# Attention and routed experts on one core: value products a slot later in the last two groups, routing of the last batch but one moved later, last tables in eight steps

## What is computed

```
x = x + (softmax(q @ k.T / sqrt(16)) @ v) @ wo.T + bo      # q from layernorm(x); k, v from ctx
z = layernorm(x)
probs = softmax((z @ Wg + bg) / 5);  vals, idx = top_k(probs, 2)
gates = vals / (sum(vals) + 1e-9), on the two experts chosen
x = x + sum_e gates[e] * (gelu(z @ W1[e] + b1[e]) @ W2[e] + b2[e])
```

## Time and profile before

| | us |
|---|---|
| three runs | 808.95, 812.42, 813.84 |
| profiled execution | 810.08, of which its span 808.4 |
| busy in the span | PE 750.2, PE weight loads 447.4, DVE 612.7, ACT 455.7, POOL 395.0 |
| attention, to the end of the last value product | about 0 to 534 |
| experts | about 535 to 808 |
| mean granted clock of PE | 0.976 of full speed |

### The profile page before, as it was taken

One profiled execution on the slowest core, in us unless ns is written; L12 is line 12 of the kernel. 1 busy time (PEld: TensorE's weight loads), 2 busy tenths in 40 slices (PEclk: granted clock), 3 DMA queues, 4 the chain that ended last, 5 costly groups with the idle time before them and its releaser, 6 DMA issues.

```text
span 808.4 us, 16197 instructions
## 1 busy us (share of the span) xinstructions
PE 750.2 (93%) x4634; PEld 447.4 (55%) x4634; DVE 612.7 (76%) x1126; ACT 455.7 (56%) x663; POOL 395.0 (49%) x357
## 2 busy tenths in 40 slices
PE   7599999999999999999999988779999989999995
PEld 3233434444443444444444433348999879998994
DVE  6786778798797788788788787556786887767774
ACT  2056766776776766776766664663345334444441
POOL 6506143647637728728725613343344455344444
PEclk9679999999999999999999999899999999999998
DMA  6766756757766757757667567775454456444441
GB/s 205 219 172 200 205 154 226 216 173 241 223 185 239 210 179 258 193 177 252 193 180 252 164 164 249 279 269 119 74 96 73 82 130 112 74 73 75 77 70 12
DMA packets 90659, 136.23 MB, mean 169 GB/s; under 512 B 15456, under 2 KB 49216, under 8 KB 90192
## 3 DMA queue, kind: packets, MB, share of 16 engines
q1 hardware_dynamic: 76592, 117.33, 48.3%
q0 software_dynamic: 13296, 17.09, 12.0%
q10 hardware_dynamic: 688, 0.79, 0.3%
HBM read 71.25 MB, written 64.04 MB: 167 GB/s over the span
## 4 chain that ended last, share of the span: by engine, by line
PE 69%; DMA 8%; DVE 8%; issue 6%; ACT 5%; POOL 2%; POOLq 1%; SPq 0%; DVEq 0%; another core or an unknown queue 0%; ACTq 0%
PE ps_pv L1536 13%; PE ring L1523 10%; PE ring L1667 9%; PE ring L1685 9%; PE ring L1510 6%; PE ps_x L1567 6%; DMA out<-y_sb,xs 6%; DVE negm L1086 4%; PE ps_x L1585 4%; PE ps_x L1577 3%; ACT probs L1014 3%; PE ring L1676 3%; PE ps_x L1595 2%; PE ps_x L1554 1%; PE ps_pv L1658 1%
## 5 line engine op out<-in xcount | busy, mean ns | idle before, releaser
L1086 DVE TENSOR_REDUCE negm<-ring 128x2 f32<-128x1024 f32 x256 | 310.4, 1223 | 76.4 <-PE ring L1510 70.7
L1014 ACT ACTIVATE probs<-ring 128x1024 f32<-128x1024 f32 x256 | 260.4, 1024 | 95.5 <-PE ring L1523 81.5
L902 POOL DMA_INDIRECT out<-y_sb,xs x71 | 110.2, 1552 | 137.8 <-DMA out<-y_sb,xs 75.2
L1536 PE MATMUL ps_pv<-probs,v_aug 128*32 128x512 f32 x1024 | 139.8, 619 | 5.5 <-ACT probs L1014 5.5
L1523 PE MATMUL ring<-kq 64*128 64x512 f32 x512 | 127.7, 498 | 8.5 <-DVE negm L1086 8.3
L1510 PE MATMUL ring<-kq 64*128 64x512 f32 x512 | 110.6, 432 | 15.2 <-ACT probs L1014 5.4
L1523 PEld LDWEIGHTS ring<-kq 64*128 64x128 f32 x512 | 48.3, 187 | 110.7 <-issue 75.6
L1047 ACT CAST xsT_hi<-ps_pv 128x256 fp32r<-128x256 f32 x70 | 26.1, 373 | 129.8 <-PE ps_pv L1658 126.0
L793 POOL DMA_INDIRECT xs_dram<-xg,rows x64 | 64.0, 1001 | 58.6 <-DVEq L1254 33.8
L1685 PE MATMUL ring<-w_hi,hT_hi 128*128 x284 | 85.3, 300 | 0.1
L1685 PE MATMUL ring<-w_lo,hT_hi 128*128 x284 | 80.1, 282 | 0.0
(11 more groups left out here) (193 smaller groups left out, 1202.4 us busy)
## 6 DMA issues: line engine op xcount, KB each, us to landing
kq<-k_dram SPq DMA_DIRECT2D x64, 192.0 KB
kq<-q_dram SPq DMA_DIRECT2D x64, 192.0 KB
xs<-xs_dram SPq DMA_DIRECT2D x71, 132.5 KB
k_dram<-qk_hi SPq DMA_DIRECT2D x32, 256.0 KB
q_dram<-qk_hi SPq DMA_DIRECT2D x32, 256.0 KB, 2.8
o_dram<-oT SPq DMA_DIRECT2D x32, 256.0 KB
w_dram<-w_sb SPq DMA_DIRECT2D x12, 512.0 KB
w_hi<-w_dram SPq DMA_DIRECT2D x12, 512.0 KB
```

Source lines behind the costliest of these rows:

```text
L902: pool.indirect_dma_start(out=out, out_offset=bass.IndirectOffsetOnAxis(ap=xs[j % AHEAD][:, TOKEN:TOKEN + 1].bitcast(I32), axis=0), in_=y_ ...
L1014: nc.scalar.activation(probs[kt][:, 2 * jp:2 * jp + 2, :], ring[PLACE["ST", u, p] % RINGS][:], ACT.Exp).then_inc(exp_done, 1)
L1086: nc.vector.tensor_reduce(negm[:, v % 2, :, jp, kt], ring[PLACE["MX", v, p] % RINGS][:], AX.X, ALU.max, negate=True).then_inc(max_free, 1)
L1536: mm = nc.tensor.matmul(ps_pv[2 * DH * j:2 * DH * (j + 1), :], v_aug[:, kt, HPG * g + j, :], probs[kt][:, j, :], start=(kt == 0), stop=(kt ...
```

## The change

1. In groups 30 and 31 the value product of key tile kt is issued at slot 2 kt + 3 (after that slot's `score_t`), and the last one at slot 1 of the next group. ACT's copy of the group's sum (`take_o`) moves with it. For group 31 the last one stays after `turn_x(0)`.
2. Batch 6: `XG0`, `XG1`, `LG` go from (2, 5), (2, 6), (2, 7) to (2, 7), (3, 0), (3, 1). The route steps go from (3, 1) to (3, 4) to (3, 4) to (3, 7), ACT's exponential of the logits from (3, 0) to (3, 3). `PX` goes from (3, 5) to turn 0 of the expert loop. `turn_x(0)` waits for `LG` in place of `PX`.
3. Batch 5 in group (0, p) of batch 7: `second` from (0, 3) to (0, 4), `gates` from (0, 4) to (0, 6).
4. `last_tables` is cut into eight parts of two to six instructions, in turns 27 to 34. Its instructions are the same.

```diff
 LAST_POST = {(1, 3): "OP0", (1, 4): "OP1", (1, 5): "OP2", (1, 6): "OP3",
-             (2, 5): "XG0", (2, 6): "XG1", (2, 7): "LG", (3, 5): "PX"}
+             (2, 7): "XG0", (3, 0): "XG1", (3, 1): "LG"}
-LAST_ROUTE = {(0, 1): "softmax", (0, 2): "first", (0, 3): "second", (0, 4): "gates"}
-LAST_ROUTE_POST = {(3, 1): "softmax", (3, 2): "first", (3, 3): "second", (3, 4): "gates"}
+LAST_ROUTE = {(0, 1): "softmax", (0, 2): "first", (0, 4): "second", (0, 6): "gates"}
+LAST_ROUTE_POST = {(3, 4): "softmax", (3, 5): "first", (3, 6): "second", (3, 7): "gates"}
-TAIL_PE = {6: "OP0", ...
+TAIL_PE = {0: "PX", 6: "OP0", ...
-TAIL_TABLES = {27: "tiles", 28: "past", 29: "rows"}
+TAIL_TABLES = {27 + n: n for n in range(8)}
+def tail_batch(j):
+    return B - 2 if j == 0 else 1 if TAIL_PE[j] == "CN" else B - 1
+def late(u):
+    return u >= G - 2
 # ACT
-                        if p == 0 and u > 0:
+                        if u > 0 and p == (1 if late(u - 1) else 0):
                             take_o(u - 1)
-                        if (g, p) == (3, 0) and i == B - 1:
+                        if (g, p) == (3, 3) and i == B - 1:
                             route_exp(i - 1)
 # PE
-                        if p == 0 and u > 0:
+                        if u > 0 and p == (1 if late(u - 1) else 0):
                             pv(u - 1, NT - 1)
-                        if p in (2, 4, 6):
-                            pv(u, p // 2 - 1)
+                        if p in ((3, 5, 7) if late(u) else (2, 4, 6)):
+                            pv(u, (p - 2) // 2)
                 if j == 0:
-                    pe.wait_ge(done["PX"], B - 1)
+                    pe.wait_ge(done["LG"], B - 1)
```

More of the change, by code:

```diff
@@ L92 @@
 TILES2 = TILES - TILES1
-TAIL_PE = {6: "OP0", 7: "OP1", 8: "OP2", 9: "OP3", 17: "XG0", 18: "XG1", 19: "LG", 25: "PX", 26: "CN"}
+TAIL_PE = {0: "PX", 6: "OP0", 7: "OP1", 8: "OP2", 9: "OP3", 17: "XG0", 18: "XG1", 19: "LG", 25: "PX", 26: "CN"}
 TAIL_LN2 = {10: "stats0", 11: "stats1", 12: "sums"}
 TAIL_ROUTE = {21: "softmax", 22: "first", 23: "second", 24: "gates"}
-TAIL_TABLES = {27: "tiles", 28: "past", 29: "rows"}
+TAIL_TABLES = {27 + n: n for n in range(8)}
 TAIL_RECIP, TAIL_NORMALISE, TAIL_APPLY, TAIL_EXP, TAIL_POW, TAIL_SCATTER = 1, 5, (15, 16), 20, 13, 25
@@ L1320, in last_tables @@
                 tiles = tile_no[:, 0:n]
-                if part == "tiles":
+                if part == 0:
                     dve.wait_ge(done["CN"], 2)
@@ L1326, in last_tables @@
                     c2.link(v.tensor_scalar(n_sh[:], n_up[:], P.bit_length() - 1, None, ALU.arith_shift_right))
+                elif part == 1:
                     c2.link(v.tensor_copy(n_tiles[:], n_sh[:]))
@@ L1330, in last_tables @@
                     c2.link(v.tensor_tensor_scan(ends[:], ones_e[:], left_n[:], 0.0, ALU.mult, ALU.add))
+                elif part == 2:
                     c2.link(v.tensor_tensor(start[:], left_n[:], ends[:], ALU.subtract))
@@ L1335, in last_tables @@
                     c2.link(v.tensor_tensor(step[:, 0:E - 1], start[:, 1:E], start[:, 0:E - 1], ALU.subtract))
-                elif part == "past":
+                elif part == 3:
                     c2.link(v.tensor_tensor(past[:, 0:n], tiles.unsqueeze(2).to_broadcast([P, n, E]), spread(ends[:], n), ALU.is_ge))
                     c2.link(v.tensor_tensor(past_n[:, 0:n], past[:, 0:n], spread(left_n[:], n), ALU.mult))
+                elif part == 4:
                     c2.link(v.tensor_reduce(e_of[:, 0:n], past[:, 0:n], AX.X, ALU.add))
                     c2.link(v.tensor_reduce(first_of[:, 0:n], past_n[:, 0:n], AX.X, ALU.add))
+                elif part == 5:
                     c2.link(v.tensor_tensor(past_n[:, 0:n], past[:, 0:n], spread(step[:], n), ALU.mult))
                     c2.link(v.tensor_reduce(start_of[:], past_n[:, 0:n], AX.X, ALU.add))
-                else:
+                elif part == 6:
                     c2.link(v.tensor_scalar(e_tab[:, TILES1:], e_of[:, 0:n], float(E - 1), None, ALU.min))
                     added_before(TILES1, n)
+                else:
                     c2.link(v.tensor_scalar(live[:], e_of[:, 0:n], float(E), None, ALU.is_lt))
@@ L1445, in tail @@
                 if j in TAIL_PE and TAIL_PE[j][:2] != "XG":
-                    misc(TAIL_PE[j], 1 if TAIL_PE[j] == "CN" else b)
+                    misc(TAIL_PE[j], tail_batch(j))
                 if j in TAIL_LN2:
@@ L1712, in _ @@
                 if j in TAIL_PE:
-                    misc(TAIL_PE[j], 1 if TAIL_PE[j] == "CN" else B - 1)
+                    misc(TAIL_PE[j], tail_batch(j))
             output(TILES - 1, e[TILES - 1])
```

## The result

The changed kernel takes 820.64 us (median of 4 runs, 819.61 to 824.5), beside 813.13 (808.95 to 816.25, 4 runs) for the kernel before on the same chip: a ratio of 1.0111, 95% interval 1.0077 to 1.0146. It is slower, by about 9 us if the ratio is applied to the time before, by 7.5 between the two medians. The forecast named 814.5, from a sum of 3.4 us lost; 820.64 lies just inside its range of 804 to 821. Sign and mechanism were right; the 3.4 us are about a third of what was lost. The profiled execution took 819.61, its span 817.9 where before's was 808.4: 9.5 us to explain.

A forecast was written before the change was run, and what follows sets the result against it. PE was taken to bound the expert stage, with a chain of adds pacing its first tiles. +4.8 (start of experts) - 0.5 (batch 5) - 2.4 (tables) + 1.5 (clock) = +3.4 us; 814.5 us named, range 804 to 821.

The forecast's parts named there:

- the start of the experts: First expert tiles: hidden(0) 2.4 us earlier, but first add late, so tiles from 4 on run 4.8 us later.
- the tables: Turns 27 to 34: the stall of 4.1 us goes, tile 36 then waits for its load; 2.4 us gained net.
- Value products: Groups 30 and 31: ACT runs through, the last product ends near 527.3 in place of 534.18, 6.9 us earlier.
- The wait for `recT`: DVE's normalise at (3, 6): DVE comes at about 523.5, recT lands at 528, hidden(0) starts at 532.6.
- PX and the scatter: Behind turn_h(0): POOL's eight scatters end at 553.3, no longer covered; the first add lands 4.8 us later.
- The clock: PE idles before hidden(0) and before the first add lands, so its clock falls: 1.5 us lost (0 to 5).
- the third rival: Start of the experts at 1.2 GHz, its loss added to the chain of adds: +9 us, 819 to 822; chance 0.21.
- Batch 5's steps: Route steps second and gates moved to later slots in batch 7's group: 0.5 us gained (0 to 1.5).
- The wait for tile 36: Expert stage behind the eight paddings: PE waits 1.6 us for the load of tile 36 (none to 2.8).
- the 4.0: Tables in eight turns: PE comes 4.0 us earlier to tile 36, before the wait for its load.
- The scatter does not set the pace: Rival at the first adds: rows come earlier or adds catch up; 5 to 6.5 us gained, 804 to 807; chance 0.14.
- all of the gain comes through: Rival at the start of the experts: no wait for recT, scatter covered; 11.5 us gained, about 800; chance 0.07.

The follow-up runs named there:

- scatter early again: Changed kernel with batch 6's PX back in the last group at (3, 7) and its route steps a slot earlier: ratio 1.0011.
- `normalise` moved: Changed kernel with batch 7's first normalise taken from slot (3, 6) to behind low_xt(1): ratio 1.0012.
- old tables: Changed kernel with the last tables in three parts again, as in the kernel before: ratio 1.0101.
- tables and paddings: Kernel before with the last tables in eight steps and the eight paddings spread two each behind the loads of tiles 36 to 39: ratio 0.9968.

## Why the prediction was wrong in size, step by step

The chain and its order were right. The steps that failed are two terms of the sum: the start of the experts, because `recT` landed later than was taken, and the tables.

**Value products: about right.** The last one was to end at 527.3 and ended at 528.78. From the last maximum on, it is 5.7 us less than before (23.9 against 29.6), where 6.9 were forecast. The experts don't get them, as said. That the products' edit alone brings these 5.7 us is not shown: in the two traces that have it without the routing edit, the last product ends 30.2 and 29.2 us after the last maximum, and both had the half clock in these groups.

**The wait for `recT`: right in kind, 2.8 us too small.** I took 528 for the landing, between bounds of 525.05 and 531.4; it was 531.07. The issue was at 525.12, 0.7 later than in the trace of before, and the 256 KB shared the engines with the 512 KB of weights issued right behind it, a store and the weight loads after that, at 291 to 416 GB/s from 528 to 536. The ground for 528, "DMA is lightly loaded just then", is the step that failed: it was true of the microsecond of the issue (131 GB/s from 524 to 528) and not of those after it. So `hidden(0)` was at 535.44, not 532.6.

**PX and the scatter: right, and the cause.** Forecast from `turn_h(0)` on: scatter 4.4 us later, first add 10.7 after it, `y_sb(4)` 14.4 after that. Measured: 542.94 to 547.35 is 4.4, then 10.3 and 14.5. Each length holds within 0.4; the chain was hung up 4.4 us too early. 2.8 of these are `recT`, the other 1.6 the half clock of `hidden(0)` and `hidden(1)` (4.36 us apart, 2.88 in before), which the sum has as a term of its own. `y_sb(4)` is 8.9 late where 4.8 and 1.5 were forecast.

**The clock: right in size, by luck in part.** It was entered once, as 1.5 us beside the chain, though I had written in the third rival that these turns are on the way to PX, the scatter and the adds. It costs 1.6 there, and only since PX stands behind them. After the stall on the first add the clock is low again (0.53 and 0.62 from 560 to 568), and no cost of that shows: from the first add to `y_sb(4)` it is 14.5 us, where 14.4 were forecast without it, and in the second trace of this kernel, at 0.55 and 0.60 from 556 to 564, `y_sb(3)` and `y_sb(4)` still waited 2.93 and 1.97 us for their adds. The third rival, 819 to 822, gave the right number, and by luck: of its 7 us of clock 1.6 are found, and what made up the rest is `recT` and the tables. The runs also show that half clock without the late scatter costs next to nothing (scatter early again, 1.0011, at 0.50 from 524 to 532). The Trainium skill, TensorE: Matmul & The Clock Gate, HAM oscillation, has each burst after a wait begin at the low clock; by this trace that holds at 535 and 561, after waits of 6.66 and 6.60 us, and it was worth some 1.6 us, not the 7 that I gave it there.

**Batch 5's steps: nothing.** Forecast 0.5 gained; alone 0.9996, and in the changed trace the last maximum is 0.3 us later than in before.

**The tables: wrong by 1.8 us.** Forecast 2.4 gained net, measured 57.02 - 56.46 = 0.6. The wait for tile 36 was right (1.6 forecast, 1.71 in the trace). What failed is the 4.0: I took a stall of 4.1 us and eight steps that hide wholly in 0.9 us a turn. PE's waits for DVE in the stretch of the tables add up to 1.07 + 1.45 + 0.90 = 3.4 in before, and 0.5 stay in the changed kernel (0.18 and 0.28), 1.1 with the paddings spread too (0.94 and 0.21). That makes 1.2 us net of the wait for tile 36; where the other 0.7 go is not shown.

**A term that was not there.** From `y_sb(5)` to `y_sb(24)` it is 72.76 us in place of 71.64, 1.1 more, of which 0.8 come at tile 6 and 0.3 at tile 7. The clock is at 1.00 through it, so that isn't the cause. The same kernel's second trace has 72.15, so some 0.6 of it differs from run to run. The rest stays open.

**The sum.** 8.9 at `y_sb(4)`, 0.5 until `y_sb(5)`, 1.1 until tile 24, -0.6 at the tables and -0.5 until the last `y_sb`, 9.5 in all (809.76 against 800.23). That is 6.1 more than the 3.4 forecast: 2.8 from the landing of `recT`, 1.8 from the tables, 0.5 from batch 5, 1.1 from the stretch without a term; the rest cancels.

**The rivals.** "The scatter does not set the pace" and "all of the gain comes through" fell at once, at the 0.30 us ahead of the first add.

## What to carry to other kernels

When work is moved behind a later stage, follow the slowest queue that it feeds to its next user: here it was not PE or DVE but POOL's order, eight scatters of 1.3 us each. They cost nothing measurable while POOL still idled ahead of the first add (4.96 us in before, 3.22 with the scatter early again), about 9 us where they ended 10 to 15 us later after the last maximum than in before, and about 1 us (1.0012) where they ended 7 us later, though right ahead of the add there too (`normalise` moved). Add every wait and every low clock that lies upstream to that chain, not beside it: here 2.8 and 1.6 us of them came through to the first add nearly in full. And when one load is moved to make room, look at what else the queue holds back: splitting the scatters freed the adds and starved tile 8.

## What the runs showed of the hardware that was not expected

**A standstill of two engines while POOL scatters.** In the first trace of the changed kernel DVE stood from 551.6 to 557.65 and ACT for 9.03 us, with their inputs from PE done by PE's records:

```profile
560.47 0.37 ACT L1058 CAST xsT_hi<-ps_pv 128x256 fp32r<-128x256 f32 x1 [9.03 <-remote]
```

DVE's ended with the scatters (547.35 to 557.3), ACT's 3.1 us behind them. "Remote" is another core or an unknown queue. The kernels with old tables and with `normalise` moved, run with the first four on the chip where before took 810.6 us, show it too (6.91 and 9.20 us; 8.14 and 9.06 us), the two with an early scatter there do not. The chip of the first trace is not known. In the twelve traces of two other chips, with the scatter late in three of them, the same time stands as a wait for the add's DMA, or isn't there. The ratio is the same with it and without it (1.0111 and 1.0094). What it is stays open; it cost nothing measurable.

**The clock in groups 30 and 31 differs from run to run.** With the same products, PE was at 0.50 from 516 to 532 in the trace of batch 5's steps alone, and at 1.00 in that of tables and paddings. The last maximum to `hidden(0)` took 32.6 us in the one, 27.6 in the other. The time of before spreads over 7 to 10 us on one chip; this may be a large part of it, which was not tried.

**An add is slower beside a large load.** With the residual's 512 KB in flight, `y_sb(3)` went 7.85 us after the add of tile 1 was issued (542.86 to 550.71); with that load later, it went 5.75 after it and without a wait. Three other traces with the load issued within 2 us of that add have 6.43 to 7.06 us; before, with the load 4.35 us ahead of the add, has 4.16. None of these runs was made to test it but the one pair.
